# A row of constants made on chip, full products in the first waits, and the pairs for the maximum set apart

## The chip, the core and the metric

The kernel runs on one core of one Trainium2 chip. A core has TensorE (matrix products), VectorE, ScalarE and GpSimd, each with a queue of its own that it works off in order, SyncE, whose queue here only starts DMAs, and 16 DMA engines. The engines wait for each other through semaphores. Times are device microseconds (us) of one execution. The figure of merit is the median over the runs: before the change 840.21 us, from three runs of 838.35 to 842.05.

## The reference

A block of a transformer on x of shape (8, 512, 128): layer norm, then attention with 16 heads of 8 columns and a mixture of 8 experts on the same normed x, and both are added to x.

```python
xn = layernorm(x)                                     # (8, 512, 128)
q, k, v = (xn @ w.T + b for each), split in 16 heads of 8
scores = q k^T * 8**-0.5, masked where xn[:, :, 0] == 0
attn = softmax(scores, axis=-1) @ v                   # 512 x 512 scores per batch and head
attention = attn @ wo.T + bo
logits = xt @ gate_w                                  # xt: the 4096 rows of xn
top 2 of 8 experts per row, weights by softmax, at most 1280 rows per expert, rank by cumsum
h = gelu(rows @ c_fc[e] + fc_bias[e]);  y = h @ c_proj[e] + proj_bias[e]
out = x + attention + weighted sum of the two y of each row
```

## The kernel before

Batches (b) have 512 rows. The front of the kernel makes, batch by batch, normed x, its transpose, q and k (128 x 512 each), v and the gate's logits. So that a product in float32r is exact enough, q and k are split in a high and a low part; the rows of a head's stack are 8 of q's parts three times over (24 rows), for k likewise. The front writes them to DRAM (`q_rows`, `k_rows`, `write_stacks`) and SyncE loads them back by quads of four heads (`load_quad`) into tiles Q[u] and K[u], where each head h of a quad has a strip of 32 partitions. Row 24 of a strip is 1 in Q and the mask in K, rows 25 and 26 are the negative maximum (high and low) in Q and 1 in K. The stacks in DRAM have all 32 rows; GpSimd fills the constant rows of all stacks by four DMAs from a tile of ones and one of zeros. K has a tile of 512 columns for each of 8 heads and is cleared by GpSimd first.

Attention works in groups: `group(b, g)`, 16 per batch, g // 8 is the half of the heads (unit), then a quad and a block of 128 keys. TensorE makes in a group four products for the scores (`scores`, L948 by the line, 27 rows of one strip, 128 keys by 512 queries, into one of three banks bX), ScalarE takes their exp (L596) into probs, and TensorE multiplies the probs of the group before with V (`with_v`, L964, eight instructions on all 128 rows, into bPV). The exp needs the maximum of each query ahead of time: for a group eight further on, TensorE makes scores with the queries as rows (`scores_for_max`, L929, in two pairs of heads, each into one of two double banks bD) and VectorE takes the maximum (`scores_max`, L738). After every fourth group the maxima are turned by TensorE (`maxima`, L938, four transposes of 8 columns), copied by ScalarE to nmT, and moved by four DMAs into the rows of Q (`max_rows`, Q<-nmT). After 8 groups the sums in bPV are copied (ScalarE, L610), turned (L973), divided (VectorE, `normalise`), turned again (`attn_turned`), copied to attnT (VectorE, L762) and multiplied by wo (`project`, L984).

The order of each engine is written out by hand in `group`, one function per engine, and the three must agree: a bank is found by counting. TensorE's `free()` waits until VectorE has left the bank used two steps ago, `next_x()` waits until ScalarE has left the one used three steps ago. Before group 0 lies a stretch (`for s in range(1, LEAD)`) with only pairs for the maximum, beside the routing of rows to experts on VectorE and GpSimd. GpSimd then waits for the first rows of maxima (s_nq), clears slot_x by ten DMAs, each waited for, and scatters xn to the experts' slots by 64 indirect DMAs (L492). Four turns of experts (two experts each) lie between the batches 3 to 7; behind the last one GpSimd gathers by 64 indirect DMAs (L510).

## Time and profile before

| | |
|---|---|
| median of 3 runs | 840.21 us |
| the profiled execution | 841.55 us |
| its span | 839.7 us |
| TensorE busy (matmul) | 611.8 us, 73% |
| VectorE busy | 423.4 us, 50% |
| ScalarE busy | 398.9 us, 48% |
| GpSimd busy | 227.1 us, 27% |
| one reduction for the maximum (VectorE, L738) | 1217 ns, 256 of them |
| one exp (ScalarE, L596) | 597 ns, 512 of them |
| mean granted TensorE clock | 0.799 of full speed |

PE is TensorE's products, PEld its loads of weights, DVE VectorE, ACT ScalarE, POOL GpSimd, SP SyncE (SPq: its queue). A row of the table of windows gives, for one stretch of the span, its length, the busy time (and number of instructions) of PE, PEld, DVE, ACT and POOL in this order, the granted TensorE clock as a share of 2.4 GHz, the share of the 16 DMA engines, and GB/s. A row of the timeline gives start, length, engine, line, operation, what it writes and reads, shapes, how many instructions are merged in it, and, in brackets, the idle time before it with what ended it. A start of a merged row is that of its first instruction. A row of the waits gives who waited for whom, the total, the number of times and the longest.

### The profile page before, as it was taken

The numbers are of one execution on the slowest core, as the hardware profiler recorded it, in microseconds if no ns is written. First come the engines' busy times: TensorE is split into PE (matmuls) and PEld (weight loads), VectorE is DVE, ScalarE is ACT, GpSimd is POOL, SyncE is SP. The second block draws the span as 40 slices with busy tenths as digits, with TensorE's granted clock in tenths as the row PEclk, the third lists the DMA queues.
The fourth block names the chain that finished last, engine by engine and source line by source line (L and its number), as shares of the span: only waits on it lengthen the run. The fifth ranks groups of instructions, "written<-read, shape, count | busy, mean of one in ns | idle before, by whom it ended". The sixth has DMA issues, their size and how long they took to land.

```text
span 839.7 us, 9577 instructions
## 1 busy us (share of the span) xinstructions
PE 611.8 (73%) x3474; PEld 304.9 (36%) x3474; DVE 423.4 (50%) x625; ACT 398.9 (48%) x773; POOL 227.1 (27%) x226
## 2 busy tenths in 40 slices
PE   1674899202299999899999999999899412079985
PEld 0442323000033333584358534863487100023322
DVE  6658855100168888516951686148713201045643
ACT  1532355100157778736784577457745200045561
POOL 5656318777200001100020002000201777730000
PEclk9966557555569999999999999999999655555775
DMA  8898142111011114102321223112312211100011
GB/s 279 245 269 246 78 182 92 54 50 53 22 44 35 52 53 139 34 32 83 113 60 33 70 90 97 32 58 61 111 51 69 76 51 50 47 26 27 2 52 50
DMA packets 61406, 68.56 MB, mean 82 GB/s; under 512 B 8496, under 2 KB 43312, under 8 KB 61360
## 3 DMA queue, kind: packets, MB, share of 16 engines
q1 hardware_dynamic: 54464, 49.86, 20.0%
q0 software_dynamic: 6896, 18.10, 6.4%
q8 instruction: 28, 0.46, 0.2%
q14 instruction: 18, 0.15, 0.1%
HBM read 33.85 MB, written 33.55 MB: 80 GB/s over the span
## 4 chain that ended last, share of the span: by engine, by line
PE 51%; DVE 14%; another core or an unknown queue 11%; ACT 10%; issue 8%; SPq 3%; DMA 2%; DVEq 0%; ACTq 0%
PE bPV L964 15%; PE bX L948 14%; PE bD L1055 9%; DVE nmax L738 8%; ACT probs L596 5%; PE bD L929 4%; ACT hid L623 3%; PE bX L938 2%; SPq L304 2%; PE bD L973 2%; PE bX L1040 1%; PE bX L1044 1%; DMA k_rows<-hid 1%; PE bX L1041 1%
## 5 line engine op out<-in xcount | busy, mean ns | idle before, releaser
L738 DVE TENSOR_REDUCE nmax<-bD 128x2 f32<-128x1024 f32 x256 | 300.2, 1217 | 192.3 <-remote 115.5
L596 ACT ACTIVATE probs<-bX 128x512 f32<-128x512 f32 x512 | 269.1, 597 | 266.4 <-PE bX L948 133.8
L948 PE MATMUL bX<-Q,K 27*128 27x512 f32 x512 | 200.0, 534 | 111.0 <-issue 75.1
L948 PEld LDWEIGHTS bX<-Q,K 27*128 27x128 f32 x512 | 81.4, 209 | 269.4 <-issue 129.8
L929 PE MATMUL bD<-K,Q 25*128 25x512 f32 x512 | 145.1, 544 | 46.1 <-DVE attn L756 28.4
L964 PE MATMUL bPV<-probs,v_aug 128*32 128x512 f32 x1024 | 164.2, 718 | 1.5 <-ACT probs L596 0.7
L500 POOL TENSOR_TENSOR wfc_hi<-wfc,ones 128x512 fp32r<-128x512 f32 x8 | 10.2, 1272 | 359.3 <-DMA pjb<-in_pjb 359.3
L929 PEld LDWEIGHTS bD<-K,Q 25*128 25x128 f32 x512 | 61.8, 213 | 81.4 <-DVE attn L756 35.5
L1055 PE MATMUL bD<-wpj,hid 128*128 128x128 f32 x640 | 74.0, 276 | 7.7 <-DVE xeT_lo L776 4.8
L1055 PEld LDWEIGHTS bD<-wpj,hid 128*128 128x128 f32 x640 | 72.4, 192 | 9.4 <-issue 9.4
L623 ACT ACTIVATE hid<-bX,fcb 128x512 f32<-128x512 f32 (+1 forms) x96 | 55.2, 614 | 27.3 <-PE bX L1044 26.6
L492 POOL DMA_INDIRECT slot_x<-xn_all,put_i x64 | 62.1, 971 | 19.4 <-issue 19.4
L786 DVE TENSOR_TENSOR ye<-bD,pjb 128x512 f32<-128x512 f32 (+1 forms) x24 | 14.4, 602 | 89.4 <-PE bD L1055 89.4
L510 POOL DMA_INDIRECT xn_all<-slot_y,get_i x32 | 32.2, 1007 | 59.5 <-DMA slot_y<-ye 50.1
L1040 PE MATMUL bX<-xeT_hi,wfc_lo 128*128 128x512 f32 (+1 forms) x96 | 35.2, 367 | 2.9 <-ACT hid L623 2.9
L964 PEld LDWEIGHTS bPV<-probs,v_aug 128*32 128x32 f32 x1024 | 21.9, 116 | 41.6 <-ACT probs L596 24.3
L510 POOL DMA_INDIRECT hid<-slot_y,get_i x32 | 32.1, 1003 | 9.8 <-issue 9.5
L1044 PE MATMUL bX<-xeT_lo,wfc_hi 128*128 128x512 f32 (+1 forms) x96 | 34.3, 357 | 0.0
L1041 PE MATMUL bX<-xeT_hi,wfc_hi 128*128 128x512 f32 (+1 forms) x96 | 34.2, 356 | 0.0
L752 DVE RECIPROCAL rsum<-bD 128x32 f32<-128x32 f32 x16 | 5.7, 356 | 55.1 <-remote 30.3
L776 DVE TENSOR_TENSOR xeT_lo<-bD,xeT_hi 128x512 fp32r<-128x512 f32 (+1 forms) x24 | 13.6, 596 | 38.4 <-ACT xeT_hi L620 38.4
L581 ACT CAST nmT<-bX 8x512 fp32r<-8x512 f32 x32 | 18.4, 574 | 27.3 <-PE bX L938 15.1
(104 smaller groups left out, 477.7 us busy)
## 6 DMA issues: line engine op xcount, KB each, us to landing
Q<-q_rows SPq DMA_DIRECT2D x32, 256.0 KB, 4.3
K<-k_rows SPq DMA_DIRECT2D x128, 64.0 KB, 3.4
slot_x<-hid POOLq DMA_DIRECT2D x10, 512.0 KB, 2.9
xe<-slot_x SPq DMA_DIRECT2D x8, 640.0 KB, 4.5
slot_y<-ye SPq DMA_DIRECT2D x8, 640.0 KB, 3.9
q_rows<-hid SPq DMA_DIRECT2D x8, 512.0 KB, 4.6
k_rows<-hid SPq DMA_DIRECT2D x8, 512.0 KB, 5.6
acc<-in_x SPq DMA_DIRECT2D x8, 256.0 KB, 8.8
```

The source lines that it names most:

```text
L492: pool.indirect_dma_start(slot_x, bass.IndirectOffsetOnAxis(ap=put_i[:, col:col + 1], axis=0), xn_all[:, n, :], None, bounds_check=SLOTS - ...
L510: pool.indirect_dma_start(gathered(b, k * TT + n), None, slot_y, bass.IndirectOffsetOnAxis(ap=get_i[:, col:col + 1], axis=0), bounds_check ...
L596: taken(nc.scalar.activation(probs[:, (g % 2) * 4 + i, :], next_x()[:], ACT.Exp, scale=SCALE))
L623: taken(nc.scalar.activation(hid[:, hc, c0:c0 + w], next_x()[:, 0:w], ACT.Gelu, bias=fcb_s[q][:, hc:hc + 1]))
L738: nc.vector.tensor_reduce(nmax[q][:, k, 2 * pair:2 * pair + 2], bank()[:], AX.X, ALU.max, negate=True).then_inc(s_dd, 1)
L929: last = nc.tensor.matmul(to[:, n, :], Q[u][rows_used, q, k * P:(k + 1) * P], K[u][rows_used, QUAD * q + h, :], start=True, stop=True)
L948: filled(nc.tensor.matmul(next_x()[:], K[u][rows_used, QUAD * q + h, j * P:(j + 1) * P], Q[u][rows_used, q, :], start=True, stop=True))
L964: last = nc.tensor.matmul(bPV[32 * h:32 * h + 32, :], v_aug[b % 2][:, j, u * UH + QUAD * q + h, :], probs[:, (g % 2) * 4 + h, :], start=(g ...
L1040: nc.tensor.matmul(to, lo, xeT[0][:, c0:c0 + w], start=True, stop=False)
L1041: nc.tensor.matmul(to, hi, xeT[0][:, c0:c0 + w], start=False, stop=False)
L1044: filled(nc.tensor.matmul(to, hi, xeT[1][:, c0:c0 + w], start=False, stop=True))
L1055: last = nc.tensor.matmul(to[:, 0, k * P:(k + 1) * P], hid[:, hc, c0 + k * P:c0 + (k + 1) * P], wpj[q][:, hc, :], start=(hc == 0), stop=(h ...
```

## The change

Four edits. The constants are no longer moved through DRAM: the stacks have 24 rows for q and 25 for k, Q and K are filled with 1 on chip at the begin, K has two blocks of 512 columns per tile, and a quad is loaded by eight DMAs (one per head and side) where it was five. In the stretch ahead of group 0 TensorE makes products of all 128 rows and 512 columns whose result nobody reads (`keep_clock`): two ahead of each pair from s = 2 on, and four ahead of group 0. In a group, the first pair for the maximum now follows the second scores and the second pair stands behind the fourth scores, and with it at the end; the turned maxima stand behind the second scores. And attnT is turned into a bank bX and copied by ScalarE, behind the third exp of group 2, where it was VectorE.

```diff
 N_CONST, N_LATER = 8, 3
-WR_DMAS, LOAD_DMAS, MAX_DMAS = 4, 5, 4
-ZERO_DMAS, ROW_DMAS = 10, 4
+WR_DMAS, LOAD_DMAS, MAX_DMAS = 4, 8, 4
+ZERO_DMAS = 10
 D_FIRST = (LEAD + 4) * 2
-D_TURN = GB * 2 + 4
+D_TURN = GB * 2 + 3
 D_EXPERTS = 2 * 2 * NCH
-assert D_FIRST % 2 == 0 and D_TURN % 2 == 0 and D_EXPERTS % 2 == 0
 D_EXPERTS_FROM = D_FIRST + EXPERTS_FROM * D_TURN + D_TURN
...
     experts_before = sum(n > (turn + 1) * GB + 3 for turn in range(EXPERTS_FROM, EXPERTS_TO))
-    return 1 + 4 * (n + 1) + (n + 3) // 4 + 2 * HC * NCH * experts_before
+    attn_turned = (n - 2) // GB if n >= 2 else 0
+    return 1 + 4 * (n + 1) + (n + 3) // 4 + attn_turned + 2 * HC * NCH * experts_before
...
-    return x_filled(0, 4 * (m - 1)) + 1 if m else 1
+    return x_filled(0, 4 * (m - 1)) + 3 if m else 1
...
-        q_rows = nc.dram_tensor("q_rows", [B, H, STRIP, T], F32, kind="Internal").ap()
-        k_rows = nc.dram_tensor("k_rows", [B, H, STRIP, T], F32, kind="Internal").ap()
+        q_rows = nc.dram_tensor("q_rows", [B, H, ROW_MASK, T], F32, kind="Internal").ap()
+        k_rows = nc.dram_tensor("k_rows", [B, H, ROW_MAX, T], F32, kind="Internal").ap()
         slot_x = nc.dram_tensor("slot_x", [SLOTS, C], F32, kind="Internal").ap()
...
-        K = [sb(f"K{u}", [P, UH, T], F32R) for u in range(UNITS)]
+        K = [sb(f"K{u}", [P, 2, T], F32R) for u in range(UNITS)]
         Q = [sb(f"Q{u}", [P, 2, T], F32R) for u in range(UNITS)]
...
                     sp.wait_ge(s_wm[b % 2], b // 2 * 16 + 16)
-                sp.dma_start(Q[u][:, q, :].bitcast(F32), q_rows[b, h0:h0 + QUAD].rearrange("h r t -> (h r) t")
-                             ).then_inc(s_load[u][q], 16)
                 for h in range(QUAD):
-                    sp.dma_start(K[u][STRIP * h:STRIP * (h + 1), QUAD * q + h, :].bitcast(F32), k_rows[b, h0 + h]
-                                 ).then_inc(s_load[u][q], 16)
+                    for tile, stack, n in ((Q[u], q_rows, ROW_MASK), (K[u], k_rows, ROW_MAX)):
+                        sp.dma_start(tile[STRIP * h:STRIP * h + n, q, :].bitcast(F32), stack[b, h0 + h]
+                                     ).then_inc(s_load[u][q], 16)
...
                 write_stacks(b, b % 2)
-            sp.wait_ge(s_rows, ROW_DMAS * 16)
-            sp.wait_ge(s_padded, UNITS)
+            sp.wait_ge(s_ones, 2 * UNITS)
             load_quad(0, 0, 0)
...
         def _(pool):
-            pool.dma_start(row_ones, tail_d[4:5, 0, :].to_broadcast([P, T])).then_inc(s_ones, 16)
-            nc.gpsimd.memset(row_zeros, 0.0).then_inc(s_fill, 1)
-            pool.wait_ge(s_fill, 1)
-            pool.wait_ge(s_ones, 16)
-            every_q, every_k = (t.rearrange("b h r t -> (b h) r t") for t in (q_rows, k_rows))
-            for stack, r0, r1, src in ((every_q, ROW_MASK, ROW_MAX, row_ones), (every_q, ROW_MAX, STRIP, row_zeros),
-                                       (every_k, ROW_MAX, NR_EXP, row_ones), (every_k, NR_EXP, STRIP, row_zeros)):
-                pool.dma_start(stack[:, r0:r1, :], src[:, None, :].to_broadcast([P, r1 - r0, T])).then_inc(s_rows, 16)
-            for u in range(UNITS):
-                nc.gpsimd.memset(K[u][:].bitcast(F32), 0.0).then_inc(s_padded, 1)
+            for tile in (*Q, *K):
+                nc.gpsimd.memset(tile[:].bitcast(F32), 1.0).then_inc(s_ones, 1)
             pool.wait_ge(s_const, N_CONST * 16)
...
                 n = b * GB + g
-                if g % 4 == 1 and not (last and g // 4 == 3):
-                    maxima(b * HALVES + g // 4 + 1, (g // 4 + 1) % 2)
                 if g == 1 and not first:
...
                         wait(act, s_pv, n - 1)
+                    if i == 2 and g % 4 == 1 and not (last and g // 4 == 3):
+                        maxima(b * HALVES + g // 4 + 1, (g // 4 + 1) % 2)
+                    if i == 3 and g == 2 and not first:
+                        take_attnT()
                     taken(nc.scalar.activation(probs[:, (g % 2) * 4 + i, :], next_x()[:], ACT.Exp, scale=SCALE))
+            def take_attnT():
+                taken(nc.scalar.copy(attnT[:], next_x()[:]))
+
             def fill_v(b):
...
                     sums(b * UNITS + 1)
+                    take_attnT()
                     return
...
-            def scores_max(s):
+            def scores_max(s, pair):
                 q, k = (s // TT) % 2, s % TT
-                for pair in range(2):
-                    take()
-                    nc.vector.tensor_reduce(nmax[q][:, k, 2 * pair:2 * pair + 2], bank()[:], AX.X, ALU.max, negate=True
-                                            ).then_inc(s_dd, 1)
-                    d.step()
-                if k == TT - 1:
+                take()
+                nc.vector.tensor_reduce(nmax[q][:, k, 2 * pair:2 * pair + 2], bank()[:], AX.X, ALU.max, negate=True
+                                        ).then_inc(s_dd, 1)
+                d.step()
+                if k == TT - 1 and pair == 1:
                     dve.wait_ge(s_dd, d.value())
...
-            def take_attnT():
-                take()
-                nc.vector.tensor_copy(attnT[:], bank()[:, 0, :]).then_inc(s_dd, 1)
-                d.step()
-
             def take_out(b):
...
             def group(b, g, last=False, first=False):
-                if not last or g + LEAD < GB:
-                    scores_max((g + LEAD) % UH)
+                ahead = not last or g + LEAD < GB
+                if ahead:
+                    scores_max((g + LEAD) % UH, 0)
                 if g == 1 and not first:
                     normalise(1)
-                if g == 2 and not first:
-                    take_attnT()
                 if g == 3 and not first:
...
                     normalise(0)
+                if ahead:
+                    scores_max((g + LEAD) % UH, 1)
-            scores_max(0)
+            for pair in range(2):
+                scores_max(0, pair)
...
             for s in range(1, LEAD):
-                scores_max(s)
+                for pair in range(2):
+                    scores_max(s, pair)
             for g in range(4):
...
                     rows_used = slice(STRIP * h, STRIP * h + NR_MAX)
-                    last = nc.tensor.matmul(to[:, n, :], Q[u][rows_used, q, k * P:(k + 1) * P], K[u][rows_used, QUAD * q + h, :],
+                    last = nc.tensor.matmul(to[:, n, :], Q[u][rows_used, q, k * P:(k + 1) * P], K[u][rows_used, q, :],
                                             start=True, stop=True)
...
-            def turned(src, n=TT):
+            def turned(src, to, n=TT):
-                to = free()
                 for k in range(n):
-                    last = nc.tensor.transpose(to[:, 0, k * P:(k + 1) * P], src(k), ident[:])
-                done(last)
+                    last = nc.tensor.transpose(to[:, k * P:(k + 1) * P], src(k), ident[:])
+                return last
...
                 pe.wait_ge(s_pvo, b * UNITS + u + 1)
-                turned(lambda k: pv_s[:, k * P:(k + 1) * P])
+                done(turned(lambda k: pv_s[:, k * P:(k + 1) * P], free()[:, 0, :]))
-            def project(since=2):
-                pe.wait_ge(s_dd, d.value(-since))
+            def project(x_since):
+                pe.wait_ge(s_xd, x.value(-x_since))
                 to = free()
...
                 pe.wait_ge(s_dd, d.value(-since))
-                turned(lambda k: attn[:, k, :])
+                filled(turned(lambda k: attn[:, k, :], next_x()))
...
+                scores(b, g, 0)
+                scores(b, g, 1)
                 if g % 4 == 1 and not (last and g // 4 == 3):
                     maxima(b * HALVES + g // 4 + 1, (g // 4 + 1) % 2)
-                scores(b, g, 0)
                 ahead(0)
-                scores(b, g, 1)
-                ahead(1)
                 scores(b, g, 2)
...
                 if g == 3 and not first:
-                    project()
+                    project(4)
                 if g == GROUPS + 1:
...
                 scores(b, g, 3)
+                ahead(1)
...
+            def keep_clock(n):
+
+                for _ in range(n):
+                    nc.tensor.matmul(bPV[:], ones_r[:], hot_f, start=True, stop=True)
+
             for s in range(1, LEAD):
+                if s == 2:
+                    pe.wait_ge(s_ranks, 1)
                 for pair in range(2):
+                    if s >= 2:
+                        keep_clock(2)
                     scores_for_max(0, 0, s, pair)
...
                     maxima(0, 0)
-            pe.wait_ge(s_ranks, 1)
+            keep_clock(4)
             for g in range(4):
```

TensorE, from the first pair for the maximum to group 0 (bD<-K,Q is a pair's product, bPV<-hot,ones_r the new full product, bX<-ident,nmhl the turned maxima), before:

```order
33 L929 MATMUL bD<-K,Q 128x512 x4
34 L1082 MATMUL bX<-hot,prefix_r 128x512
35 L1083 MATMUL bPV<-hot,ones_r 128x512
36 L929 MATMUL bD<-K,Q 128x512 x20
37 L938 MATMUL bX<-ident,nmhl 8x128 x4
38 L929 MATMUL bD<-K,Q 128x512 x8
39 L948 MATMUL bX<-Q,K 128x512
```

and after, the last rows of the same place:

```order
51 L1076 MATMUL bPV<-hot,ones_r 128x512 x2
52 L918 MATMUL bD<-K,Q 128x512 x2
53 L927 MATMUL bX<-ident,nmhl 8x128 x4
54 L1076 MATMUL bPV<-hot,ones_r 128x512 x2
55 L918 MATMUL bD<-K,Q 128x512 x2
...
60 L1076 MATMUL bPV<-hot,ones_r 128x512 x2
61 L918 MATMUL bD<-K,Q 128x512 x2
62 L1076 MATMUL bPV<-hot,ones_r 128x512 x4
63 L937 MATMUL bX<-Q,K 128x512 x2
```

Seven such cycles of two full products and a pair stand between the first of them and the last pair ahead of the turned maxima, four more behind.

TensorE in a group with turned maxima and sums (group 9 of batch 0; bX<-Q,K are scores, bPV<-probs the product with V), before:

```order
95 L948 MATMUL bX<-Q,K 128x512
96 L938 MATMUL bX<-ident,nmhl 8x128 x4
97 L948 MATMUL bX<-Q,K 128x512
98 L929 MATMUL bD<-K,Q 128x512 x2
99 L948 MATMUL bX<-Q,K 128x512
100 L929 MATMUL bD<-K,Q 128x512 x2
101 L948 MATMUL bX<-Q,K 128x512
102 L964 MATMUL bPV<-probs,v_aug 32x512 x4
103 L973 MATMUL bD<-ident,pv_s 128x128 x4
```

and after:

```order
115 L937 MATMUL bX<-Q,K 128x512
116 L918 MATMUL bD<-K,Q 128x512 x2
117 L937 MATMUL bX<-Q,K 128x512 x2
118 L927 MATMUL bX<-ident,nmhl 8x128 x4
119 L918 MATMUL bD<-K,Q 128x512 x2
120 L937 MATMUL bX<-Q,K 128x512
121 L953 MATMUL bPV<-probs,v_aug 32x512 x4
122 L961 MATMUL bD<-ident,pv_s 128x128 x4
```

The second pair of a group now stands between the last scores of it and the first of the next, and the turned maxima behind two of the group's own scores. On ScalarE (bX<-exp into probs, pv_s the copy of the sums) the same place moved from

```order
84 L581 CAST nmT<-bX 8x512
85 L610 COPY pv_s<-bPV 128x512
86 L596 ACTIVATE probs<-bX 128x512 x8
87 L605 COPY v_aug<-v_all 128x8x4x8 x2
```

to

```order
85 L602 COPY pv_s<-bPV 128x512
86 L585 ACTIVATE probs<-bX 128x512 x2
87 L568 CAST nmT<-bX 8x512
88 L585 ACTIVATE probs<-bX 128x512 x5
89 L588 COPY attnT<-bX 128x512
90 L585 ACTIVATE probs<-bX 128x512
91 L597 COPY v_aug<-v_all 128x8x4x8 x2
```

The copy of the sums stands first now, and two exps stand ahead of the copy of the maxima.

## Rows read from the trace of the kernel before

**Rows 1.** Table of windows, whole span by regimes (columns as explained above).
```profile
17.38:67.85 50.47, 35.16 (x128) 21.83 (x128) 29.92 (x99) 21.96 (x64) 29.21 (x25) 0.86 0.88 264
67.85:94.38 26.53, 13.39 (x38) 5.09 (x39) 25.75 (x42) 3.73 (x7) 16.22 (x26) 0.51 0.50 153
94.38:136.71 42.33, 40.81 (x170) 13.00 (x172) 25.16 (x28) 23.17 (x45) 14.45 (x12) 0.50 0.39 151
...
144.40:226.60 82.20, 13.48 (x47) 4.14 (x43) 7.32 (x6) 6.44 (x11) 56.09 (x58) 0.54 0.16 52
...
245.94:652.00 406.06, 382.18 (x2548) 218.50 (x2546) 244.60 (x299) 269.35 (x507) 23.31 (x19) 1.00 0.23 67
```

**Rows 2.** Timeline of the start, and one fill by GpSimd.
```profile
7.94 1.66 POOL L411 DMA_DIRECT2D k_rows<-probs  x2
8.03 9.21 DVE L673 TENSOR_SCALAR xn_all<-acc,mv,rstd 128x128 f32<-128x128 f32 x4
9.60 6.98 POOL L413 MEMSET K<- 128x4096 f32 x2
...
17.38 1.09 PE L886 MATMUL bX<-ident,xn_all 128*128 128x128 f32 x4 [17.38 <-DVE xn_all L673]
...
25.98 1.40 DVE L673 TENSOR_SCALAR xn_all<-acc,mv,rstd 128x128 f32<-128x128 f32 x4
...
89.33 0.95 POOL L480 MEMSET hid<- 128x1024 f32 x1
```

**Rows 3.** DMA issues of the page: count, KB each, us to landing.
```profile
Q<-q_rows SPq DMA_DIRECT2D x32, 256.0 KB, 4.3
K<-k_rows SPq DMA_DIRECT2D x128, 64.0 KB, 3.4
```

**Rows 4.** Timeline of TensorE between the front and group 0.
```profile
74.37 0.63 PE L1083 MATMUL bPV<-hot,ones_r 128*128 128x512 f32 x1
74.93 0.79 PE L929 MATMUL bD<-K,Q 25*128 25x512 f32 x2
...
79.28 0.80 PE L929 MATMUL bD<-K,Q 25*128 25x512 f32 x2 [2.52 <-DVE nmax L738]
...
87.75 0.79 PE L929 MATMUL bD<-K,Q 25*128 25x512 f32 x2 [0.34 <-DVE nmax L738]
88.47 1.01 PE L938 MATMUL bX<-ident,nmhl 128*8 128x128 f32 x4
...
94.38 0.76 PE L948 MATMUL bX<-Q,K 27*128 27x512 f32 x1 [0.93 <-DMA Q<-nmT]
```

**Rows 5.** Timeline: products with V of groups 0 and 11.
```profile
99.17 1.94 PE L964 MATMUL bPV<-probs,v_aug 128*32 128x512 f32 x8
...
143.43 1.07 PE L964 MATMUL bPV<-probs,v_aug 128*32 128x512 f32 x8
```

**Rows 6.** Table of windows, single groups and the stretch ahead of 136.71.
```profile
103.23:107.29 4.06, 3.81 (x17) 0.99 (x16) 2.35 (x3) 2.07 (x6) 0.53 (x1) 0.50 0.42 173
133.62:136.71 3.09, 3.09 (x16) 1.09 (x17) 2.18 (x3) 1.14 (x3) 2.91 (x2) 0.50 0.04 11
270.88:273.47 2.59, 2.52 (x17) 0.82 (x16) 2.52 (x5) 2.06 (x6) 0.00 (x0) 1.00 0.09 6
273.47:276.65 3.18, 3.12 (x21) 1.20 (x21) 2.09 (x3) 2.64 (x7) 0.00 (x0) 1.00 0.53 160
284.45:287.76 3.31, 3.17 (x22) 1.23 (x21) 2.21 (x3) 2.78 (x7) 0.00 (x0) 1.00 0.51 152
287.76:291.05 3.29, 3.23 (x21) 1.37 (x21) 3.26 (x6) 2.48 (x6) 0.00 (x0) 1.00 0.02 5
```

**Rows 7.** Timeline of an ordinary group behind the product with V at 270.88.
```profile
272.40 2.06 ACT L596 ACTIVATE probs<-bX 128x512 f32<-128x512 f32 x4 [0.53 <-PE bX L948]
...
273.05 0.49 PE L948 MATMUL bX<-Q,K 27*128 27x512 f32 x1
```

**Rows 8.** Waits, whole span.
```profile
ACT probs L596 <- remote: 116.5, 13, 28.1
```

16 lines of the change are left out of this document (6 added, 10 removed).

## The prediction, made before the result was known

> **What bounds the kernel now.** I first cut the span into stretches with the table of windows, then followed the timeline through each, then read the waits. The reader is to see in [rows 1] that the granted clock of TensorE stands at the lower of its two levels (0.50, 1.2 GHz) from 94.38 to 136.71, and near it from 144.40 to 226.60, a stretch in which TensorE is busy for only 13.48 of 82.20 us. There GpSimd issues indirect DMAs, and ScalarE waits for something that the profile calls remote, 116.5 us in all, here and in a like stretch near the end [rows 8]. Only some three groups of scores get done in it. The change leaves the indirect DMAs alone, and a group needs as many hand-overs from TensorE as before. So I treat these two starved stretches as fixed in length and in work done.
>
> Outside them there are three regimes. From 17.38 to 67.85 it is the DMA engines: their share is 0.88 at 264 GB/s, and no other engine is busy for more than 35.16 of 50.47 us [rows 1]. From 67.85 to 94.38 it is VectorE, busy for 25.75 of 26.53 us. From 94.38 on it is a chain: product with V, last scores, exp, third scores, product with V. An ordinary group takes 4.06 us at 1.2 GHz and 2.59 us at 2.4 GHz [rows 6].
>
> **The start.** VectorE's normalisation of the first batch starts at 8.03 and lasts to 17.24. GpSimd issues row DMAs beside it from 7.94 and clears the padded K tiles from 9.60 to 16.58, and TensorE starts at 17.38 [rows 2]. Four such operations took 1.40 us at 25.98, so without GpSimd's work beside them they end near 9.4. After the change GpSimd has 4 tiles of 128x1024 to fill ahead of everything else; one such fill took 0.95 us [rows 2], 3.8 us together, done well ahead of 8.03. TensorE starts 8.0 us earlier. If VectorE was held by something else (loads of x in flight), the start stays where it is.
> The stage behind it is bound by DMA, so it keeps its length and moves with its start, but for the loads. A quad of heads was 256 + 4x64 = 512 KB in 5 loads [rows 3]; it is 4x48 + 4x50 = 392 KB in 8. Below: 120 KB less at 264 GB/s is -0.45 us. Above: the loads of K now have 25 rows, which 16 queues can't share evenly; a quad that moved at half the rate would cost its old time once more, 512 KB at 264 GB/s, +1.9 us. One quad lies ahead of the last stack that the stage waits for. I take +1.0, nearer the upper end, since the queues are full there. What the removed row DMAs cost is in the 8.0 already. Sum: -7.0 us, between -4 and -9. The Trainium skill (DMA: Bandwidth & Descriptors, Why a DMA increments its semaphore by 16 and not by 1) says that a DMA runs on the largest number of engines up to 16 that divides its rows: 5 for 25 rows, 12 for 24. By it engines 0 to 4 would carry 56 KB of a quad for 32 KB before, an estimated +1.5 us here. No row of this trace shows it.
>
> **The full products in the first waits.** Two 128x512 products stand ahead of each of 12 pairs and four ahead of group 0, 28 in all. From a full product to a pair in strips took 0.56 us, and from a pair in strips to an operation of all 128 rows 0.72 us [rows 4]; from one full product to the next I take the same 0.56, at least 0.43 (512 columns at 1.2 GHz). A cycle of pair, product, product is then 1.84 us, at least 1.71, against VectorE's 1.2 for its pair. So TensorE becomes the bound of this stage. Seven cycles lie between the pair at 79.28 and the last pair ahead of the turned maxima: 79.28 + 7x1.84 + 0.72 = 92.9 for 88.47, +4.4 (+3.5 at the shorter cycle). Eleven cycles, the maxima and the last four products lie ahead of group 0: 79.28 + 11x1.84 + 0.85 + 0.72 + 3x0.5 + 0.56 = 103.2 for 94.38, +8.8 (+7.0 at the shorter cycle). The rows of the maxima, which group 0 waited for before (5.9 us behind 88.47), are then no longer late. I take +4.0 for the maxima and +8.2 for group 0. Group 0 starts at 94.38 - 7.0 + 8.2 = 95.6, and the indirect DMAs, which wait for the maxima's rows and then for ten fills, start 7.0 - 4.0 = 3.0 us earlier.
>
> **Does the clock rise from it?** Ahead of the rise at 136.71 TensorE went from a product with V straight into full 128x128 transposes and was busy for 3.09 of 3.09 us [rows 6]. In the 42 us of groups at 1.2 GHz before that it was busy for 40.81 us, nearly half of that in the product with V (1.94 of 4.06 us), the rest in strips, and did not rise [rows 1, 5, 6]. In the new cycle the two full products make 0.85 of 1.84 us, 46%, about the same part, and each change of shape leaves a gap. So I forecast that it stays at 1.2 GHz up to the same places as before.
>
> **The groups.** Ordinary: from a product with V the first exp starts 1.52 us later, the third scores 0.65 behind it, the next product with V 0.42 behind those: 2.59 [rows 7]. The new order keeps this chain: no change. With turned maxima (groups 5 and 13 of a batch, 3.18 us [rows 6]): they move behind the second scores and so wait for the first exp, and then the pair and the third scores start together: 1.52 + 0.65 + 0.51 (half of the 1.01 at 1.2 GHz [rows 4]) + 0.42 = 3.10, -0.08. Groups 1 and 9 (3.31): ScalarE now copies the sums ahead of the exp on which the third scores wait, two more steps of 0.49: 1.52 + 0.65 + 0.98 + 0.42 = 3.57, +0.26. The next one (3.29) loses the wait for the normalisation between its pairs, at most -0.12. The copy of attnT goes from VectorE to ScalarE, beside an exp whose scores are not ready: nothing. Per batch 2x0.26 - 2x0.12 - 2x0.08 = +0.12; over 7 batches +1 us.
>
> **The sum.** Group 11's product with V stood at 143.43, 1 us ahead of the starved stretch [rows 5]. After, the stretch begins at 141.4. Group 0's product with V is at 95.6 + 4.8 = 100.4 (99.17 - 94.38 before), and group 9's, with 4.06 us per group and two of 5.04 (with maxima), at 100.4 + 7x4.06 + 2x5.04 = 138.9, since the groups that ran at 2.4 GHz from 136.71 are hardly reached. It stands 2.5 us ahead of the stretch, 0.6 of a group, where group 11's was 0.4 of one ahead. So 1.8 groups fewer are done, and they are made up behind it at 4.06 us: +7.3. The stretch ends 3.0 earlier. 7.3 - 3.0 + 1.0 = +5.3 us. The profiled execution took 841.55 us (span 839.7), 1.3 above the median of 840.2: 841.55 + 5.3 - 1.3 = 845.5, and I say 845. This case alone reaches from 838 to 853: 3 us from the start, 2 from the cycle, 4 from where the clock rises and how many groups pass the starved stretches.
>
> **Rivals.**
> First, the other side: the full products lift the clock before group 0 and the groups hold it, as they held it from 245.94 to 652 [rows 1]. For it: full products without a gap stood ahead of the rise. Against it: the gaps, and the 46%. It decides once the granted clock is 1.0 at group 0. Then the cycles get short (about +2), the groups ahead of the starved stretch take some 2.8 us, five more are done at its begin (4.06 us each behind it before), and it ends 5 earlier: -25 if the clock rises again at the sums of the next group 9, -11 if only a batch later. Middle -18, with the median 822 us. The Trainium skill (TensorE: Matmul & The Clock Gate, What's actually happening) has sustained matmul activity release the lower clock; read simply, the time is this rival's. The 42 us at 0.50 with TensorE nearly always busy speak against so simple a reading [rows 1].
> Second, the products cost only about +3, since strips and full products may overlap better than in these few rows. Then start and products nearly cancel against the lost groups: 840 us.
> Third, setting the pairs apart shortens the groups with maxima: VectorE was busy for only 2.09 of 3.18 us in one [rows 6], and if 0.4 us comes back in each of 28 it is -11: 834 us.
> Fourth, the clock rises later than before behind the first starved stretch, at the sums of a group 9 in place of those of the batch's begin; nine groups at 4.06 - 2.59 = 1.47 us more are +13: 858 us.
>
> **Chances.** Forecast 0.48, first 0.20, second 0.12, third 0.12, fourth 0.08. A difference of 0.5%, 4.2 us, is about what can be told from none. Faster: 0.20, 0.10 of the third, 0.02 of the forecast: 0.32. Same (836 to 844.4): 0.10 of the second, 0.13 of the forecast, 0.02 of the third: 0.25. Slower: the rest, 0.43. The range leaves out half of the first rival below and most of the fourth above: 823 to 855.
>
> **What would show it.** TensorE's first transposes near 9.4 (start right) or near 17 (wrong). Pairs 1.7 to 1.9 us apart with VectorE idle between them (cycle right), or 1.1 to 1.3 (second rival). Group 0 near 95.6. A granted clock of 0.50 from there to the first starved stretch (forecast) or of 1.00 (first rival). Groups of 2.59, 3.10 and 3.57 us at the upper clock. The forecast is wrong if the clock is up at group 0, or if group 0 starts before 92.

## The result and the profile after

The changed kernel took 864.12 us (median of four runs, 848.81 to 876.16) where before took 839.83 (838.35 to 842.05). The ratio is 1.020, 95% interval 1.012 to 1.028: slower beyond the noise, though whether by as much as 2% is not settled, and outside the range of 823 to 855. The ratios here leave out runs more than 1.5% above the fastest of the same kernel; in this case those are mostly the runs with the lower mean granted clock, so the medians of all runs stand beside them. The profiled execution, the slowest of the four, took 876.16 us (span 874.3) for 841.55 before: its 34.6 us are more than the 24.3 between the medians.

The start and the pairs' stage came out as forecast. Timeline of TensorE, VectorE and GpSimd, the first rows, then one cycle and the last pair ahead of group 0:

```profile
7.67 1.08 PE L875 MATMUL bX<-ident,xn_all 128*128 128x128 f32 x4 [7.67 <-DVE xn_all L666]
...
6.41 1.12 DVE L666 TENSOR_SCALAR xn_all<-acc,mv,rstd 128x128 f32<-128x128 f32 x4
...
0.74 1.84 POOL L400 MEMSET Q<- 128x1024 f32 x2 [0.29 <-POOLq L1138]
...
78.75 0.79 PE L918 MATMUL bD<-K,Q 25*128 25x512 f32 x2
79.48 1.22 PE L1076 MATMUL bPV<-hot,ones_r 128*128 128x512 f32 x2
80.63 0.79 PE L918 MATMUL bD<-K,Q 25*128 25x512 f32 x2
...
83.22 1.01 PE L927 MATMUL bX<-ident,nmhl 128*8 128x128 f32 x4
...
93.37 0.80 PE L937 MATMUL bX<-Q,K 27*128 27x512 f32 x3
```

VectorE's normalisation takes 1.12 us where it took 9.21 [rows 2]; pairs are 1.88 us apart; group 0 starts at 93.37, and its groups run at 0.50 up to the starved stretch, as forecast (second row below).

What was not forecast stands in the tables of windows. First the changed kernel: the stage of the pairs, the groups ahead of the starved stretch, then 244 to 538; then batch 4 to 5 and 5 to 6, each from the product with V of a group 2 to the next such, with a turn of experts in it:

```profile
57.94:93.37 35.43, 28.35 (x67) 12.24 (x67) 27.46 (x44) 3.74 (x7) 17.45 (x28) 0.52 0.35 117
93.37:131.96 38.59, 35.31 (x147) 10.21 (x146) 23.45 (x19) 21.74 (x43) 13.12 (x9) 0.50 0.37 145
...
243.99:479.51 235.52, 214.81 (x1448) 116.72 (x1446) 147.02 (x178) 157.02 (x300) 10.12 (x8) 0.99 0.19 55
479.51:537.54 58.03, 54.93 (x232) 15.93 (x232) 33.65 (x36) 30.04 (x58) 5.09 (x4) 0.50 0.21 61
...
433.75:542.22 108.47, 100.56 (x546) 51.94 (x545) 49.73 (x60) 57.09 (x106) 5.09 (x4) 0.73 0.18 51
542.22:638.28 96.06, 89.08 (x545) 50.88 (x544) 49.51 (x60) 56.67 (x106) 5.07 (x4) 0.88 0.20 58
```

and the same two turns of the kernel before:

```profile
428.07:514.63 86.56, 81.18 (x545) 49.10 (x544) 48.27 (x61) 55.80 (x105) 5.07 (x4) 1.00 0.24 70
514.63:601.19 86.56, 81.17 (x545) 49.08 (x544) 48.27 (x61) 55.79 (x105) 5.05 (x4) 1.00 0.24 70
```

At the product with V of group 2 of batch 4 the changed kernel is 433.75 - 428.07 = 5.7 us late, about the +5.3 of the forecast (the 0.99 of the row up to 479.51 is a dip of the clock from 278.1 to 281.5). The next two turns add 21.9 and 9.5 us, with the granted clock at 0.73 and 0.88 for 1.00. Behind them it is 37.1 us late, 38.2 behind the second starved stretch (778.82 for 740.59) and 34.7 at the last product with V. So 31 of the 34.6 us lie where [rows 1] had the clock at 1.00 from 245.94 to 652.

Three of its falls (479.5, 588.7, 684.3) lie in the group behind a turn of experts, where TensorE now idles longer. Windows of the changed kernel, each from one product with V to the next: an ordinary group, one with maxima, group 9 and the one behind it, and the one behind a turn of experts (twice: at 1.00 throughout, and where the clock falls at 479.5), then the next ordinary group:

```profile
322.38:324.98 2.60, 2.60 (x17) 0.84 (x16) 2.36 (x3) 2.07 (x6) 0.00 (x0) 1.00 0.08 9
324.98:328.21 3.23, 2.69 (x21) 0.92 (x20) 3.00 (x5) 2.69 (x7) 0.00 (x0) 1.00 0.38 112
336.01:339.58 3.57, 3.03 (x21) 1.10 (x21) 3.24 (x6) 3.04 (x8) 1.19 (x1) 1.00 0.96 262
339.58:342.77 3.19, 2.88 (x22) 1.19 (x21) 2.45 (x5) 2.00 (x6) 3.03 (x4) 1.00 0.29 90
...
388.55:392.93 4.38, 3.49 (x22) 1.28 (x21) 2.45 (x2) 4.37 (x8) 0.00 (x0) 1.00 0.67 197
476.32:481.40 5.08, 4.22 (x22) 1.48 (x20) 2.45 (x2) 4.80 (x8) 0.00 (x0) 0.81 0.66 181
481.40:485.46 4.06, 3.81 (x19) 0.99 (x16) 2.16 (x2) 1.97 (x5) 0.00 (x0) 0.50 0.11 41
```

Before, behind the experts, the same place was:

```profile
384.07:387.66 3.59, 3.31 (x22) 1.29 (x21) 2.32 (x3) 3.58 (x8) 0.00 (x0) 1.00 0.90 266
```

The period of a group hardly changed, but a group with maxima now leaves TensorE idle for 3.23 - 2.69 = 0.54 us, where it was busy for 3.12 of 3.18 [rows 6]. Behind the experts the idle time went from 0.28 to 0.89 us. The timeline of that place shows why: ScalarE loads its table at 388.47, the second pair now stands behind the last scores, and the turned maxima behind two scores more, so all of it waits for the first exps.

```profile
388.47 1.28 ACT L585 ACT_TABLE_LOAD   x1 [8.69 <-PE bX L937]
388.55 1.07 PE L953 MATMUL bPV<-probs,v_aug 128*32 128x512 f32 x8
...
389.76 3.05 ACT L585 ACTIVATE probs<-bX 128x512 f32<-128x512 f32 x6
390.41 0.49 PE L937 MATMUL bX<-Q,K 27*128 27x512 f32 x1 [0.80 <-ACT probs L585]
...
391.97 0.60 PE L927 MATMUL bX<-ident,nmhl 128*8 128x128 f32 x4
392.50 0.50 PE L918 MATMUL bD<-K,Q 25*128 25x512 f32 x2
```

### The profile page after: what moved, and what is told of

It is laid out like the page before. It is cut to its first block, busy times and chain, and to the rows that moved or that the text cites. A ratio compares the mean times of both kernels' runs of the same rounds, so it can differ in the third digit from the quotient of the medians.

```text
span 874.3 us, 9722 instructions
## 1 busy us (share of the span) xinstructions
PE 649.2 (74%) x3502; PEld 310.0 (35%) x3502; DVE 421.6 (48%) x617; ACT 404.1 (46%) x781; POOL 220.2 (25%) x222
## 4 chain that ended last, share of the span: by engine, by line
PE 57%; another core or an unknown queue 14%; ACT 10%; DVE 7%; issue 5%; DMA 2%; SPq 2%; POOL 1%; DVEq 0%; POOLq 0%; ACTq 0%
PE bPV L953 18%; PE bX L937 13%; PE bD L1043 8%; ACT probs L585 6%; PE bD L918 6%; PE bX L927 3%; ACT hid L615 3%; DVE nmax L730 2%; PE bPV L1076 2%; PE bD L961 2%; DMA k_rows<-hid 2%; PE bX L1028 1%; PE bX L1032 1%; PE bX L1029 1%
## 5 line engine op out<-in xcount | busy, mean ns | idle before, releaser
L730 DVE TENSOR_REDUCE nmax<-bD 128x2 f32<-128x1024 f32 x256 | 306.1, 1221 | 256.7 <-remote 131.6
L585 ACT ACTIVATE probs<-bX 128x512 f32<-128x512 f32 x512 | 272.8, 601 | 294.0 <-PE bX L937 148.0
L937 PE MATMUL bX<-Q,K 27*128 27x512 f32 x512 | 174.6, 605 | 104.7 <-issue 74.0
L953 PE MATMUL bPV<-probs,v_aug 128*32 128x512 f32 x1024 | 182.4, 794 | 0.7 <-ACT probs L585 0.7
L918 PE MATMUL bD<-K,Q 25*128 25x512 f32 x512 | 169.5, 566 | 18.0 <-DVE nmax L730 11.1
L937 PEld LDWEIGHTS bX<-Q,K 27*128 27x128 f32 x512 | 65.4, 219 | 277.0 <-issue 147.0
L918 PEld LDWEIGHTS bD<-K,Q 25*128 25x128 f32 x512 | 69.3, 232 | 55.3 <-DVE nmax L730 24.2
L927 PE MATMUL bX<-ident,nmhl 128*8 128x128 f32 x128 | 26.1, 343 | 53.6 <-ACT probs L585 27.2
L927 PEld LDWEIGHTS bX<-ident,nmhl 128*8 128x8 f32 x128 | 10.6, 96 | 72.3 <-issue 66.5
L1029 PE MATMUL bX<-xeT_hi,wfc_hi 128*128 128x512 f32 (+1 forms) x96 | 34.7, 361 | 0.0
```

Source lines behind the costliest of these rows:

```text
L585: taken(nc.scalar.activation(probs[:, (g % 2) * 4 + i, :], next_x()[:], ACT.Exp, scale=SCALE))
L730: nc.vector.tensor_reduce(nmax[q][:, k, 2 * pair:2 * pair + 2], bank()[:], AX.X, ALU.max, negate=True).then_inc(s_dd, 1)
L918: last = nc.tensor.matmul(to[:, n, :], Q[u][rows_used, q, k * P:(k + 1) * P], K[u][rows_used, q, :], start=True, stop=True)
L927: last = nc.tensor.transpose(to[0:8, k * P:(k + 1) * P], nmhl[q][:, k, :, :].rearrange("p h s -> p (h s)").bitcast(F32), ident[:])
L937: filled(nc.tensor.matmul(next_x()[:], K[u][rows_used, q, j * P:(j + 1) * P], Q[u][rows_used, q, :], start=True, stop=True))
L953: last = nc.tensor.matmul(bPV[32 * h:32 * h + 32, :], v_aug[b % 2][:, j, u * UH + QUAD * q + h, :], probs[:, (g % 2) * 4 + h, :], start=(g ...
```

## The experiments

Where before took about 670 to 684 us (all but e5 to e8), the waits called remote are absent: there GpSimd's indirect DMAs starve nobody. The table gives medians of all runs, the median of before beside it on the same chip, and the ratio with its 95% interval. For e1 to e3 the ratio is that of the medians, without an interval. The two kinds of ratio differ by up to 2%, so kernels are compared below by one kind at a time.

| run | median (range) | before | ratio |
|---|---|---|---|
| e1_order_back | 682.5 (657.4 to 684.4) | 681.3 | medians 1.002 |
| e2_no_products | 701.4 (681.5 to 716.2) | 681.3 | medians 1.030 |
| e3_order_only | 732.6 (710.2 to 740.8) | 681.3 | medians 1.075 |
| e4_rows_only | 658.7 (656.1 to 669.9) | 681.3 | 0.982 (0.977 to 0.986) |
| e5_maxima_late | 888.0 (867.0 to 930.7) | 840.4 | 1.037 (1.030 to 1.043) |
| e6_pairs_apart | 875.9 (871.0 to 905.8) | 840.4 | 1.040 (1.035 to 1.044) |
| e7_lift | 819.8 (817.5 to 833.3) | 840.4 | 0.976 (0.972 to 0.980) |
| e8_rows_products | 840.1 (828.8 to 864.4) | 840.4 | 0.997 (0.993 to 1.001) |
| e9_changed_again | 717.0 (689.9 to 749.6) | 682.3 | 1.038 (1.020 to 1.056) |
| e10_changed_held | 676.6 (666.8 to 695.3) | 682.3 | 1.003 (0.997 to 1.010) |
| e11_best | 663.0 (660.9 to 688.7) | 682.3 | 0.992 (0.988 to 0.996) |
| e12_full_each | 680.4 (669.2 to 699.8) | 682.3 | 1.008 (1.002 to 1.013) |
| e13_changed_pieces | 700.9 (689.6 to 702.8) | 683.2 | 1.045 (1.039 to 1.052) |
| e14_best_pieces | 647.1 (645.4 to 650.5) | 683.2 | 0.966 (0.959 to 0.973) |
| e15_rows_again | 662.8 (656.8 to 672.0) | 683.2 | 0.981 (0.976 to 0.985) |

**Which edit costs.** e1 sets the order of a group back in the changed kernel, e3 changes only it in the kernel before; e2 leaves out the products, e4 has only the rows.

In `group` of TensorE for e1, with VectorE and ScalarE alike, and then e2:

```diff
+                if g % 4 == 1 and not (last and g // 4 == 3):
+                    maxima(b * HALVES + g // 4 + 1, (g // 4 + 1) % 2)
                 scores(b, g, 0)
+                ahead(0)
                 scores(b, g, 1)
-                if g % 4 == 1 and not (last and g // 4 == 3):
-                    maxima(b * HALVES + g // 4 + 1, (g // 4 + 1) % 2)
-                ahead(0)
+                ahead(1)
                 scores(b, g, 2)
...
                 scores(b, g, 3)
-                ahead(1)
```

```diff
-                    if s >= 2:
-                        keep_clock(2)
...
-            keep_clock(4)
```

> The changed kernel with the order inside a group as before: both pairs for the maximum between the first three scores, the turned maxima ahead of the first scores; rows on chip, full products and the copy of attnT on ScalarE stay. In the changed kernel's trace the clock of TensorE fell to 0.50 at 479.5 and stayed there to 537.5, and again at 588.7, 619.5 and 684.3, where before it stood at 1.00 from 245.94 to 655.5. Theory A (the new order leaves TensorE idle longer behind the experts and in the groups, 4.38 us from product with V to product with V behind the first experts for 3.59 before, and so the clock falls): no fall between the two starved stretches here, 838 to 846 us, the runs within 4 us of each other, 3.6 us at that place. Theory B (the other order is innocent; the front made 9.7 us shorter and the full products only put every group at another time against the moments at which the chip changes the clock, so that falls come or don't): falls stay, 850 to 876 us, with a scatter of over 10 us.

> The changed kernel without its 28 full products ahead of group 0 (the two that rank the experts' rows stay). Both theories: the pairs are 1.2 us apart again and group 0 starts near 86 in place of 93.4. Theory A (order): falls of the clock between the starved stretches stay, 845 to 870 us with scatter. Theory B (shift in time and the products): the falls are fewer or gone, near 838. What the products cost by themselves, apart from falls: between 0 and 7 us.

> The kernel before with only the order inside a group changed (first pair behind the second scores, turned maxima behind them too, second pair behind the last scores; attnT stays on VectorE, no full products, rows through DRAM). Theory A: falls of the clock between the starved stretches, 850 to 870 us, runs over 10 us apart, 4.4 us behind the first experts. Theory B: no falls, 838 to 843 us. Between them: if the order costs only its 0.26 us per group with sums, 841 to 843 with the clock at 1.00 throughout.

> The kernel before with only the constant rows made on chip and the quads loaded by eight DMAs of 24 and 25 rows. Both theories: TensorE starts near 7.7 as in the changed kernel, 9.7 us earlier than before, and group 0 near 85 to 87. Theory A: no falls of the clock, time 829 to 838 us (what of the 9 us is left behind the starved stretches). Theory B: the shift in time brings falls, 845 us and more in some runs.

Theory A held. With the order set back the clock stayed at 1.00 from 173.6 to 648.0. The order alone made the slowest kernel of the four, its fastest run (710.2) 26 us above the slowest of before (684.3), with the clock down from 258.7 to 262.2, from 313.4 to 371.4 and again behind each further turn of experts. e2, whose group 0 began at 83.7, rose at 90.5 without any added product and fell again all the same (394.3 to 452.3 and 592.2 to 650.3 among others). e4 rose at 125.0 and held to 616.5: the shift in time alone brought no fall. Windows of e3, behind the experts and the stretch that follows:

```profile
310.25:315.33 5.08, 4.27 (x23) 1.48 (x21) 2.45 (x2) 4.80 (x8) 0.00 (x0) 0.81 0.74 221
315.33:360.00 44.67, 42.23 (x183) 11.87 (x180) 26.02 (x28) 23.22 (x45) 0.00 (x0) 0.50 0.21 61
```

All four missed in level, being expected for a before of 840; what counts is the distance from before. Of e1 it is none by the medians, as expected, though its runs lie 27 us apart where 4 were expected. Of e3 it is 51 us where 10 to 30 were expected.

**Which half of the order.** e5 moves only the turned maxima behind the second scores, e6 only sets the pairs apart.

```diff
-                if g % 4 == 1 and not (last and g // 4 == 3):
-                    maxima(b * HALVES + g // 4 + 1, (g // 4 + 1) % 2)
                 scores(b, g, 0)
                 ahead(0)
                 scores(b, g, 1)
+                if g % 4 == 1 and not (last and g // 4 == 3):
+                    maxima(b * HALVES + g // 4 + 1, (g // 4 + 1) % 2)
                 ahead(1)
```

```diff
                 scores(b, g, 0)
-                ahead(0)
                 scores(b, g, 1)
-                ahead(1)
+                ahead(0)
                 scores(b, g, 2)
...
                 scores(b, g, 3)
+                ahead(1)
```

> The kernel before with only the turned maxima moved behind the second scores of their group (the copy of them on ScalarE behind the second exp); both pairs for the maximum stay between the first three scores. The run with the whole order changed took 732.6 us for 681.3 of before on the same chip, with nine stretches at 0.50 behind the first rise. Theory A1 (it is the moved maxima, which leave TensorE idle in a group that has them): most of the 50 us is here, and the clock falls behind the experts, where a group with maxima stands. Theory A2 (it is the pair set behind the last scores): 0 to 3 us over before, no falls between the batches.

> The kernel before with only the two pairs for the maximum set apart (first behind the second scores, second behind the last scores), the turned maxima first in their group as before. Theory A1: within 3 us of before, no falls. Theory A2: most of the 50 us, with falls of the clock in ordinary groups and behind the experts. If both e5 and e6 cost part, the two idle times add up, and the clock falls only where both meet.

Neither A1 nor A2: each alone costs 4%. Nor does the clock fall only where both meet, the third case that e6 named. Windows of e5 and of e6 at 1.00, a group with maxima and the one behind the experts:

```profile
464.90:468.37 3.47, 2.94 (x22) 1.05 (x21) 2.99 (x4) 2.94 (x7) 0.00 (x0) 1.00 0.47 145
433.42:437.44 4.02, 3.73 (x22) 1.40 (x21) 3.23 (x4) 4.01 (x8) 0.00 (x0) 1.00 0.88 265
```

```profile
330.03:333.43 3.40, 3.34 (x22) 1.20 (x21) 3.33 (x6) 2.64 (x7) 0.00 (x0) 1.00 0.52 158
394.27:398.52 4.25, 3.45 (x22) 1.37 (x20) 2.59 (x3) 4.24 (x8) 0.00 (x0) 1.00 0.77 231
```

Each stretches these two kinds of group by 0.2 to 0.7 us (3.18 and 3.59 before) for the same products. Not each makes TensorE idle in both: e6's group with maxima is idle for 0.06 us, as before, and e5's group behind the experts for 0.29, where before it was 0.28, and yet the clock fell at the end of just this group. So idle time by the profile's count doesn't account for every fall. e5 had 0.50 in 256.5 to 321.4, in 335.0 to 389.6 and behind the experts at 437.4, 533.0 and 628.6, e6 behind those at 486.4, 582.0 and 677.6.

**Products elsewhere.** e7 is e4 with a burst ahead of group 0 and two products in each of the last eight groups; e8 is e4 with the 28 products of the change.

```diff
                     elif not last:
                         scores_for_max(b + 1, 0, head - GB, pair)
+                    else:
+                        nc.tensor.matmul(free()[:, 0, :], ones_r[:], hot_f, start=True, stop=True)
...
+            keep_clock(16)
             for g in range(4):
                 group(0, g, first=True)
```

> The kernel before with rows made on chip (656 to 670 us where before took 670 to 684) and full products put elsewhere: 16 without a gap ahead of group 0, and one in place of each missing pair in the last eight groups. If the clock is lifted by full products that follow each other without strips and gaps between them, it is at 1.00 from group 0 on, where e4 had 0.50 up to 125.0, and stays up to the end, where e4 had 0.50 from 616.5: nine groups at 2.6 for 4.06 us and six more at the end, -22 us, less about 5 for the burst: 640 us where e4 has 657. If not even that lifts it: +5 us and the falls as in e4.

> The kernel before with rows made on chip and the 28 full products of the changed kernel ahead of group 0; order of the groups and copy of attnT as before. e1, which has the copy of attnT on ScalarE besides, took 682 us and stood at 0.50 up to 173.6; e4, without both, took 657 and rose at 125.0. Theory P (the products delay group 0 by 7 us and the rise of the clock to a later group with sums): near 680, group 0's scores near 93, the rise behind 140. Theory S (it is ScalarE's copy): near 660 to 665, the rise near 132.

e7 took 2.4% less than before. Timeline of its burst:

```profile
83.11 6.34 PE L1077 MATMUL bPV<-hot,ones_r 128*128 128x512 f32 x16
89.37 0.49 PE L935 MATMUL bX<-Q,K 27*128 27x512 f32 x1
```

The clock rose at 88.3, within it, and an ordinary group took 2.60 us from the first on. It was down again from 125.8 to 224.8, behind a cast of VectorE that took 6.74 us from 122.79 (more on it below) and through the starved stretch. How much of the 2.4% is the rows, how much the burst and how much the last groups was not separated.

The 28 products of the change, more than the 16 of the burst but spread in twos between pairs, lifted nothing for long: e8 had 0.50 up to 242.7 but for 92.5 to 95.9. Its expected times were for a before of 681 and can't be read here. What can be read fits Theory P: group 0's scores at 92.6, a late rise, and no copy of attnT on ScalarE to explain it, for a net of nothing (0.997). ScalarE's copy costs 0.06 us a batch (groups of 3.25 for 3.19 in e1) and no more. But e1 and e8 both have a cast of 6.88 us at 123.68, and e4 has none. What the products cost by their delay and what by where they put this cast is not separated.

**Is it the clock or the waits?** e9 is the changed kernel again. e10 adds work to it, full products just in the groups that idle.

It is in `scores_for_max`, called with `full` as `g % 4 == 1 or g == 4`:

```diff
                 to = free()
+                if full:
+                    nc.tensor.matmul(to[:, 0, :], ones_r[:], hot_f, start=True, stop=True)
```

> The changed kernel itself, beside e10 on the same chip. Where GpSimd's indirect DMAs starve TensorE (before at 840) it should take 849 to 876 us as it did; where they don't (before at 670 to 684) 690 to 740 us, as the order alone took 733 there, the rows give back 10 to 13 and the products cost up to 10. In both: falls of the clock behind the experts.

> The changed kernel with one full product of 128 rows ahead of each pair for the maximum in five of 16 groups: those with turned maxima (g = 1, 5, 9, 13) and g = 4, the first one behind the experts. It adds work and takes no wait away. Theory A (the time is lost through the clock, which falls because the new order leaves TensorE idle longer in just these groups): the clock stays at 1.00 from the first rise to the second starved stretch or the last groups, and the time is 10 to 30 us below e9. Theory C (the waits of the new order cost by themselves, and the clock is a symptom): no gain; 10 products of 0.2 to 0.45 us per batch make it 15 to 30 us longer.

> The kernel before with rows made on chip, 16 full products without a gap ahead of group 0, and one (where e7 had two) in each of the last eight groups. e7 took 819.8 us for 840.4 of before; its last groups took 3.13 us at 1.00 with two products, 4.06 at 0.50 without. With one: near 2.7 us each if the clock stays up, 3 us below e7 (0.972 of before); if one isn't enough to hold it, 4.06 and up to 6 us above e7.

> As e11, and one full product ahead of the first pair of every group besides, 120 in all. If they fit into idle time of TensorE: groups stay at 2.60 us and the clock comes back sooner where it was down. If they don't: each costs 0.2 to 0.45 us at 1.00, 25 to 50 us in all, and the gain in clock can't pay for it.

Adding ten products per batch made it 40 us faster by the medians (717.0 to 676.6), 3.3% by the ratios (1.038 to 1.003). Windows of e10: all between the rise and the last groups, and batch 4 to 5 from group 2 to group 2:

```profile
136.54:597.33 460.79, 426.09 (x2883) 239.47 (x2880) 283.87 (x343) 308.89 (x580) 95.76 (x93) 1.00 0.23 67
351.32:439.70 88.38, 81.48 (x556) 49.95 (x555) 48.14 (x60) 56.70 (x106) 5.05 (x4) 1.00 0.22 63
```

88.38 us for 86.56 before: with the clock held, the new order and the added products cost 1.8 us a turn. The changed kernel's 108.47 and 96.06 hold the rest, 20 and 8 us, which is the clock. Theory C is out.

Behind the experts e10's group took 3.98 us, idle for 0.25, but a group with maxima kept its 0.54 us of idle time (2.91 busy of 3.45) at a clock of 1.00. Not all of the 40 us lie behind the experts: e10's clock rose at 136.5 and e9's at 173.6, an estimated 13 us (nine groups at 2.60 for 4.06), and that may be the cast of the next paragraphs, 4.86 us in e9 and 0.90 in e10.

e12, with a product in every group, shows that the products are not free: groups of 2.61, 2.86 and 2.95 us for 2.60, and 17 us over e11. Nor did they hold the clock at the start: in e12 it rose in the burst at 85.2 and was down again from 92.1 to 174.0.

e11 held its last groups at 2.61 us with one product each (4.06 in e4), but lost the burst's gain at another place: its ratio is 0.992, that of the rows alone 0.982 (e4). Timelines of VectorE and GpSimd in e11:

```profile
121.90 7.29 DVE L730 CAST nmhl<-nmax 128x16 fp32r<-128x16 f32 x1
...
120.30 8.86 POOL L474 TENSOR_TENSOR acc<-acc,bo_s 128x4096 f32<-128x4096 f32 x1 [3.48 <-DMA slot_x<-hid]
```

A cast of 16 columns took 7.29 us beside GpSimd's one long addition, TensorE waited for the maxima behind it, and the clock fell from 127.1 to 164.6. In the changed kernel it is there too, and the reduction ahead of it, under the same addition (123.10 to 131.96), took its usual 1.23 us:

```profile
126.74 1.23 DVE L730 TENSOR_REDUCE nmax<-bD 128x2 f32<-128x1024 f32 x1 [1.70 <-PE bD L918]
128.00 3.99 DVE L735 CAST nmhl<-nmax 128x16 fp32r<-128x16 f32 x1
```

The kernel before has no such cast, because its addition (127.52 to 136.37) lies between two casts (125.97 and 142.40), as it does in e4 and e15. The long casts end with the addition: in e11 at 129.19 for 129.16, in e2 at 128.74 for 128.71. In e10 the cast began 0.87 us ahead of the end of the addition, and took as long:

```profile
130.18 0.90 DVE L735 CAST nmhl<-nmax 128x16 fp32r<-128x16 f32 x1
...
122.18 8.87 POOL L474 TENSOR_TENSOR acc<-acc,bo_s 128x4096 f32<-128x4096 f32 x1 [2.44 <-DMA slot_x<-hid]
```

**The cast.** e13 is the changed kernel, e14 is e11, both with the addition in eight pieces between the clearing DMAs; e15 is e4 again.

```diff
             for h in range(ZERO_DMAS):
                 pool.dma_start(...).then_inc(s_zero, 16)
+                if h < B:
+                    part = nc.gpsimd.tensor_tensor(rows(acc, h), rows(acc, h), bo_s[...], ALU.add)
...
                 pool.wait_ge(s_zero, h * 16 + 16)
-            nc.gpsimd.tensor_tensor(acc[:], acc[:], bo_s[...], ALU.add).then_inc(s_bo, 1)
```

> The changed kernel with GpSimd's addition of bo to acc (one instruction of 8.86 us between the tenth clearing DMA and the scatter) cut in eight of 1.1 us, each issued while GpSimd waits for a clearing DMA. Theory D (VectorE's cast is held up by the long addition beside it; the stall of TensorE behind it withholds the rise of the clock at the sums of batch 0): no cast over 1.3 us there, the scatter starts 8.9 us earlier, and the clock rises near 140 where e9 had 0.50 up to 173.6; 5 to 20 us below e9. Theory E (the cast waits for something else, or the order alone withholds the rise): a cast stays long or the rise stays at the next batch, and only the 8.9 us of earlier scatter are won, of which little reaches the end. The falls behind the experts stay in both.

> e11 (rows on chip, 16 full products ahead of group 0, one in each of the last eight groups) with the addition cut in eight. In e11 the cast at 121.90 lasted 7.29 us, the product with V behind it came 9.94 us after the one before, and the clock fell to 0.50 from 127.1 to 164.6. Theory D: no stall, the clock at 1.00 from 86 to the end, -7 us for the stall and -1.46 for each of ten groups: 640 us where e11 has 663; where GpSimd starves TensorE, only 5 to 10 us below e7. Theory E: as e11.

> The same kernel as e4 (rows made on chip, nothing else), beside e14. On a chip without starved stretches 656 to 670 us as before; on one with them 9 us of the front against what the starved stretches take back: 832 to 840 for 840. It serves as the measure of what the burst and the full products in the last groups are worth in e14.

For the casts Theory D held in both, for the time in e14 alone. The longest cast near there was 1.56 us in e13, the clock rose at 136.4 (173.6 in the profiled execution of e9), and falls behind the experts stayed (307.0 to 327.5 and 402.6 to 423.1). But the ratio of e13 is 1.045 where e9 has 1.038, so a gain in time doesn't show there (the medians, 1.026 and 1.051 of before, point the other way). e14 is the best kernel, 5% below before by the medians and 3.4% by the ratio, and 16 us below the rows alone by the medians (an estimated 10 by the ratios, 0.966 and 0.981); it was expected at 640 us and took 647. Its windows, the pairs' stage, all that follows, one of the last groups:

```profile
57.98:85.28 27.30, 15.64 (x41) 7.11 (x42) 26.52 (x41) 2.69 (x7) 17.05 (x28) 0.50 0.42 133
85.28:624.58 539.30, 508.84 (x3319) 266.26 (x3317) 348.30 (x445) 369.30 (x701) 158.94 (x159) 1.00 0.26 77
610.20:612.80 2.60, 2.60 (x15) 0.89 (x14) 2.56 (x11) 2.07 (x6) 1.99 (x3) 1.00 0.78 214
```

It was not run where GpSimd starves TensorE.

## Why the prediction was wrong

**The start: right in its cause, 2.9 us short in size.** -9.7 at the first transposes and -9.9 at the first pair (57.94 for 67.85), for -8.0 and, with +1.0 for the loads, -7.0, outside the -4 to -9 of the sum; the fills took 3.7 us. The normalisation was not only shorter but began 1.6 us earlier (6.41 for 8.03), behind x's data, which VectorE had sooner; this I had at nothing. The stage bound by DMA lasted 50.27 us for 50.47, so my +1.0 for the loads doesn't show. Neither does the estimated +1.5 by the Trainium skill (DMA: Bandwidth & Descriptors, Why a DMA increments its semaphore by 16 and not by 1), by which a DMA of 25 rows runs on 5 engines.

**The products: right.** Cycles of 1.88 us for 1.84. With the start's 9.9 us added back, the maxima were turned at 93.1 (forecast 92.9) and group 0 began at 103.3 (103.2). The clock stayed at 0.50 through both, as forecast; the first rival is out for these products, and e7 shows what it would have taken. The second is out too: the cycle of 1.88 us is as long as the sum that lets full products and strips overlap no more than in [rows 4].

**The lost groups: right, with luck in one part.** Group 9's product with V stood at 139.22 (forecast 138.9), but only because two misses met. Group 0's stood at 98.22 for 100.4, by the earlier start, and the nine groups behind it took 41.0 us for 38.5: 1.3 by the stalled cast ahead of group 8 (6.44 for 5.10), which was not in the sum, and 1.0 by group 9, put at 4.06 and measured at 5.10. Two groups fewer were done at the end of the starved stretch, for 1.8, and that end came 3.8 us earlier (224.21 for 227.98), for 3.0. Together group 14's product with V came 4.35 us later (232.33 for 227.98), for 7.3 - 3.0 = 4.3.

**The groups: right in length, and here is the step that failed.** 2.60, 3.23, 3.57 and 3.19 us for 2.59, 3.10, 3.57 and 3.17; a batch without experts took 47.70 us for 47.26 (298.31 to 346.01, before 294.24 to 341.50), +0.4 where I had +0.12. But the part on the groups took [rows 1]'s clock of 1.00 from 245.94 to 652 as given, and asked only how the new order changes the period. It did not ask how close the kernel stood to losing it, and it never priced the group behind the experts (3.59 to 4.38 us). The order left TensorE's period alone and took away its cover, and the clock fell there: +31 us in two turns of this execution, more or fewer in others. e3 against before and e1 against e9 show that it is the order, e10's turn of 88.38 us at 1.00 that it is the clock. The third rival, that the order shortens groups with maxima, had the wrong sign (3.23 for 3.18). The fourth named the clock, but as one late rise behind the starved stretch, for +13; the rise there came at 244.0 for 245.9, and the place was +4.4 at most (group 15 of batch 0 at 236.39 for 232.04).

That small waits make the clock swing is also what the Trainium skill tells of another kernel (TensorE: Matmul & The Clock Gate, A second HAM failure mode: psum-queue depth-cycling), and this trace agrees: the single wait behind the experts was 0.80 us. The prediction used the page for its rule on rising alone (What's actually happening). That rule, sustained activity releases the clock, holds for e7's burst and not for the 42 us of groups at 0.50 [rows 1].

**What stays open.** Why the fall comes behind one turn of experts and not behind another (at 479.5, not at 388.6, with the same 0.8 us of idle time) was not separated; the times of one kernel scatter by it. Neither was how much idle time is too much, or whether idle time is the right measure at all: e5 lost the clock behind the experts at an idle time as before (0.29 us for 0.28), and e10 held it with 0.54 us idle in its groups with maxima. Shown is that the order brings the falls and that added full products stop them. Nor is it known what makes GpSimd's indirect DMAs starve TensorE in some sessions and not in others.

## What to carry to other kernels

Before moving work of an engine whose clock follows its load, sum its idle time per place and not only the length of the chain: an order with the same period and more idle time can cost more than any wait in it. Idle time is a warning and not a measure (e5); the test is a run with products added (e10). A clock at the upper level for 400 us says nothing of its margin; look at the thinnest place, here the group behind a table load. To raise the clock, put full products without a gap ahead of the work that needs it: 16 raised it in all four kernels that had them, 28 in twos between strips did not. It stayed up in e14 alone; e7 and e11 lost it behind the long cast, e12 within 7 us. To hold it, a few in the groups that idle do, in every group they cost more than they bring.

## What the hardware showed besides

A 16-column cast on VectorE took up to 8.1 us (e2) while GpSimd ran one 8.86 us addition, and 1.56 or less beside 1.3 us pieces; a reduction from PSUM under the same addition kept its 1.23 us. The normalisation at the start looks like the same case, though no run separates it: 9.21 us beside GpSimd's row DMAs and fills, 1.12 without. The cast agrees with the Trainium skill (SBUF — State Buffer, SBUF: two separate sides), by which VectorE and GpSimd share a pair of ports that one instruction holds to its end.

The kernel before took 840 us by the median in two sessions and 681 to 683 in three, and one chip showed both (832 to 867 us beside e5 to e8, 670 to 698 beside e13 to e15). In the latter no wait of the profile is called remote, and the 64 indirect DMAs run beside groups of 2.60 us. The first rows of ScalarE's waits in e15:

```profile
ACT probs L583 <- PE bX L935: 105.3, 126, 4.6
ACT L583 <- PE bX L935: 34.8, 4, 8.7
```

The 116.5 us of [rows 8], and the low clock around them, belong to the session and not to the program. A change that is judged beside them should be measured where they are absent too.
